# A conv, dynamic-filter and expert block on one core: the matmuls that only keep TensorE busy are taken out

## The reference

```python
x = x + conv_block(layernorm_over_channels(x))
t = tokens(x)
t = t + experts(layernorm(t))
return from_tokens(t)

def conv_block(x):                       # 128 -> 32 -> 128 channels
    xd = relu(group_norm(conv1x1(x, w_scale1)))
    outs = []
    for w, d in zip((w_cata, w_catb, w_catc, w_catd), (1, 4, 8, 12)):
        f = softmax(conv3x3(xd, w, dilation=d), axis=1)       # 9 weights a pixel
        outs.append(sum(shifted(xd, k, d) * f[:, k] for k in range(9)))
    y = relu(group_norm(conv1x1(concat([xd] + outs), w_scale2)))
    return relu(group_norm(conv1x1(y, w_scale3)))

def experts(t):                          # 8 experts, the best 2 for each token
    w, i = top_2(t @ gate_w.T); w = softmax(w)
    return sum over the 2 chosen e of w * (gelu(t @ w1[e].T + b1[e]) @ w2[e].T + b2[e])
```

## Time and profile before

| | |
|---|---|
| median of 3 runs | 345.13 us (343.13 to 347.28) |
| profiled execution | 345.51 us, its span 343.7 us |
| mean granted TensorE clock | 0.903 |
| busy in the span: TensorE, VectorE, ScalarE, GpSimd | 285.0, 182.2, 149.4, 204.6 us |
| matmuls with line L1181 | 66, of 379 to 635 ns each by the trace |

### The profile page before, as it was taken

How to read it: one execution, slowest core, us unless ns; L and a number is a source line. 1 busy time by engine, 2 the same in 40 slices (tenths; PEclk the granted TensorE clock), 3 DMA queues, 4 the chain that set the end, 5 groups by cost and what they waited for, 6 DMA issues and landing times.

```text
span 343.7 us, 4640 instructions
## 1 busy us (share of the span) xinstructions
PE 285.0 (83%) x1446; PEld 200.4 (58%) x1446; DVE 182.2 (53%) x429; ACT 149.4 (43%) x352; POOL 204.6 (60%) x195
## 2 busy tenths in 40 slices
PE   2999979877998664747999999999999999993054
PEld 0245525242343344516898888888888888882032
DVE  3673699999794788989953111121112222312086
ACT  2742321211003578366936655544554454343082
POOL 9300269696870036077576777777777777765271
PEclk9999999996899686668999999999999999998555
DMA  7100000000000003375435556665666556630585
GB/s 298 64 3 0 2 0 0 0 2 0 0 0 2 2 0 154 104 281 168 153 109 167 178 178 173 204 207 178 180 205 200 180 176 210 196 109 31 208 352 188
DMA packets 13768, 41.79 MB, mean 122 GB/s; under 512 B 3121, under 2 KB 3121, under 8 KB 13745
## 3 DMA queue, kind: packets, MB, share of 16 engines
q1 hardware_dynamic: 8640, 29.52, 26.3%
q0 software_dynamic: 4096, 8.40, 7.7%
q10 hardware_dynamic: 1008, 3.59, 2.6%
HBM read 32.05 MB, written 9.44 MB: 121 GB/s over the span
## 4 chain that ended last, share of the span: by engine, by line
PE 63%; DVE 24%; POOL 4%; issue 3%; ACT 3%; DMA 2%; DVEq 0%; POOLq 0%; SPq 0%; ACTq 0%
PE PS L1367 20%; PE PS L1378 20%; PE PS L1242 6%; DVE PRF L846 4%; PE PS L1228 3%; PE PS L1189 3%; POOL RX L451 2%; DVE PRF L1144 2%; DVE st L897 2%; PE PS L1356 2%; PE PS L1389 2%; PE PS L1334 2%; PE PS L1181 1%; DMA SCR<-expert_rows 1%; DVE FE L823 1%
## 5 line engine op out<-in xcount | busy, mean ns | idle before, releaser
L681 ACT ACTIVATE MV<-PS,WE 128x256 f32<-128x256 f32 x156 | 61.1, 474 | 57.5 <-PE PS L1367 57.5
L506 POOL DMA_INDIRECT expert_rows<-RX,dsti x64 | 62.5, 977 | 25.1 <-issue 16.9
L1367 PE MATMUL PS<-SCR,WE 128*128 (+1 forms) x312 | 75.6, 386 | 0.0
L1378 PE MATMUL PS<-MV,WE 128*128 128x256 f32 x312 | 73.7, 379 | 0.0
L458 POOL TENSOR_TENSOR PRF<-PRF 128x1024 f32<-128x1024 f32 x21 | 49.4, 2359 | 40.2 <-DVE PRF L846 38.7
L1378 PEld LDWEIGHTS PS<-MV,WE 128*128 128x128 f32 x312 | 59.0, 190 | 7.8
L1367 PEld LDWEIGHTS PS<-SCR,WE 128*128 128x128 f32 x312 | 57.3, 193 | 6.9 <-issue 0.3
L1104 DVE TENSOR_SCALAR PRF<-PS,WE 128x256 f32 x30 | 14.5, 485 | 80.5 <-PE PS L1378 80.5
L499 POOL DMA_INDIRECT RX<-token_rows,dsti x46 | 44.1, 959 | 14.0 <-issue 13.7
L846 DVE TENSOR_TENSOR PRF<-RX,PS 128x512 f32<-128x512 f32 x66 | 41.7, 677 | 6.0 <-PE PS L1228 5.9
L1228 PE MATMUL PS<-FT,k 72*128 72x512 f16 x72 | 27.4, 403 | 5.2 <-DVE PRF L846 3.6
(11 more groups left out here) (235 smaller groups left out, 376.8 us busy)
## 6 DMA issues: line engine op xcount, KB each, us to landing
WE<-experts SPq DMA_DIRECT2D x39, 514.5 KB
token_rows<-SCR SPq DMA_DIRECT2D x4, 512.0 KB, 3.2
SCR<-expert_rows SPq DMA_DIRECT2D x4, 512.0 KB, 8.1
SCR<-expert_rows ACTq DMA_DIRECT2D x4, 512.0 KB, 8.4
out<-PRF SPq DMA_DIRECT2D x8, 256.0 KB, 2.2
X<-x ACTq DMA_DIRECT2D x2, 512.0 KB, 6.3
X<-x SPq DMA_DIRECT2D x2, 512.0 KB, 8.2
first_token_rows<-SCR SPq DMA_DIRECT2D x2, 512.0 KB, 2.6
```

The lines of the kernel that those rows point to most:

```text
L506: nc.gpsimd.indirect_dma_start(yr, bass.IndirectOffsetOnAxis(ap=dsti[:, 1, q:q + 1].bitcast(U32), axis=0), YS[:, q % NR, :], None).then_in ...
L681: last = nc.scalar.activation(GF[:, j % 2, c * STEP:(c + 1) * STEP], first_layer(j, c), ACT.Gelu, bias=part(j, "b1")[:, c:c + 1])
L1367: last = nc.tensor.matmul(first_layer(j, c), part(j, "w1")[:, c * P:(c + 1) * P], columns, start=True, stop=True)
L1378: last = nc.tensor.matmul(second_layer(j), part(j, "w2")[:, c * C:(c + 1) * C], GF[:, j % 2, c * STEP:(c + 1) * STEP], start=(c == 0), sto ...
```

## The change

All four calls of `keep_busy` and the function itself are taken out; 66 matmuls go. Nothing else changes, and no other instruction changes its order on its engine.

```diff
             per_image(2, WC1[:, :], X, u_done)
 
-            def keep_busy(n, b):
-
-                for _ in range(n):
-                    nc.tensor.matmul(bank(b), k16_("ident"), k16_("sel")[:, 0:HALF], start=True, stop=True)
-
             def logits(d, tap):
...
             pe.wait_ge(c16_in, 16)
-            keep_busy(30, 6)
             pe.wait_ge(wcb_ready, 2 * B)
...
                     if d + 2 < ND and LOGITS_AT[tap] == at:
                         logits(d + 2, tap)
 
-            keep_busy(12, 5)
 
             def third_conv(b, h, first):
...
             nc.tensor.matmul(bank(4, 2 * B), prm_("group"), mv3[:, 0:2, :], start=True, stop=True).then_inc(gm_done, 1)
-            keep_busy(12, 5)
             tokens(0)
             tokens(1)
...
                 one_hot(i + 1, OHQ_A, i, 2 * i, bank(4, 2 * QA), i == 0, i == 1)
-            keep_busy(12, 7)
 
             def ranks():
```

## The result

| | before | after |
|---|---|---|
| median | 345.02 us (4 runs, 343.13 to 347.28) | 348.63 us (4 runs, 346.25 to 349.80) |
| profiled execution, its span | 345.51, 343.7 us | 347.94, 346.1 us |
| mean granted clock | 0.903 | 0.874 |

The ratio is 1.0105 (95% interval 1.0060 to 1.0151, which is 2.1 to 5.2 us): slower by 3.6 us, with 3.0 forecast and 348.1 us against 348.6. The ratios given here leave out executions that lie over 1.5% above the fastest of their kernel (four of the 12 in e1, e5 and e9); their mean granted clock is 0.866 to 0.883, against 0.878 to 0.898 in the others of these three, and that is a part of what is measured, so for the experiments the mean of all executions stands beside the ratio, with twice its standard error.

A forecast was written before the change was run, and what follows sets the result against it. TensorE was taken to bound the experts' stage, so earlier delays add one for one. 1.9 + 0.4 + 0.7 + 0 = +3.0 us on the profiled 345.5 gives 348.5; the median is 0.4 lower, so 348.1 us, range 345.8 to 351.0.

The forecast's parts named there:

- What bounds, and that nothing swallows a delay: Experts, 160 to 310 us: TensorE busy 149.96 of 150 us, so any earlier delay enters the result one for one.
- Place 1: 30 matmuls before the 3x3 convolution: without them the clock falls and the convolution starts at 0.50; +1.9 us (1.3 to 2.7).
- Place 2: 12 matmuls before the third convolution: without them the clock falls before or inside it, even chances; +0.4 us (0 to 0.9).
- Place 3: 12 matmuls before the tokens: without them tokens start sooner, near 118.4 us, but at 0.50; +0.7 us (-0.3 to +2.3).
- Place 4: 12 matmuls before the gather wait and experts: nobody waits for them and the clock falls anyway; 0 us.
- The sum: All four removals together: +3.0 us, giving 348.1 us, 0.9% slower; chance 0.60.
- Time freed at place 3: Rival: place 1's idleness costs no lasting clock, and tokens' statistics start 0.8 us sooner; 344.3 us, chance 0.14.
- The clock low for longer: Rival: late rises, place 2's full 0.9 and place 3 at 0.50 throughout; +5.9 us, 351.0 us, chance 0.14.
- Place 4 holding the clock: Rival: the block before the experts keeps the clock up in most executions; +1.8 us, 349.9 us, chance 0.07.
- The collision of VectorE with GpSimd's addition: Rival: shifted work shrinks or grows a 2.00 us VectorE step; at most 1.7 us either way, 346.4 if gone, chance 0.05.

The follow-up runs named there:

- e1: Kernel before with only the 30 warming matmuls in front of the 3x3 convolution removed; +2.2 +- 1.5 us, ratio 1.0023.
- e5: Kernel before with 10 instead of 30 warming matmuls at the same point ahead of the 3x3 convolution; +2.1 +- 1.5 us, ratio 1.0032.
- e9: Kernel before with the 30 warming matmuls ahead of the 3x3 convolution replaced by 60 of 32 columns; +1.5 +- 1.4 us, ratio 1.0005.
- e12: The changed kernel again, all four warming blocks out, against the kernel before, in 12 executions; +2.7 +- 0.9 us, ratio 1.0084, median 348.12 us.
- e3: Kernel before with only the 12 warming matmuls in front of the tokens removed; +2.3 +- 1.2 us, ratio 1.0075.
- e11: Kernel before with the 12 warming matmuls behind the one-hot products removed and one added behind each of 10 broadcasts; -1.8 +- 0.7 us, ratio 0.9952.

## Why the prediction was right

**What bounds, and that nothing swallows a delay.** Right. The 1.5 us of place 1 was 1.6 at the third convolution and, with place 3's 1.5 added, 3.0 at the experts; Route is 29.3 to 29.7 us in every profile.

**Place 1, +1.9 (1.3 to 2.7).** Right. The three profiles without the block (after, e1, e12) have Conv 1.5, 2.8 and 1.4 us later, mean 1.9; e1's lies 0.1 above the range. That the mean is the forecast's own figure is luck, with three values that far apart. The clock fell as forecast, 3.9 us after the last matmul in the changed kernel.

**Place 2, +0.4 (0 to 0.9).** Right in both ends: 0, 0 and 0.8 us in three profiles. The even chances can't be told better with three.

**Place 3, +0.7 (-0.3 to +2.3).** The mechanism was right (start at 118.4 less shift, at 0.50, the statistics waiting for TensorE), the size too small: 1.5 us between the two profiles, 1.4 between the averages. Two parts of the term were off. The rise in the changed kernel's first profile came 5.9 us behind the tokens' start, later than any of the three rises that I took the 2.6 to 5.4 us from; in e3 and e12 it was 4.6 and 3.6 us, inside them. And the block was judged by one execution, in which it ran at 0.50 to its end; in seven of ten a part of the block ran at 1.00, it was over in 4.2 to 4.4 us instead of 5.3, and Tokens took 14.1 to 14.2 us, 0.9 less than in the profile from which I had made the sum. Against that one profile the three without the block are 1.5, 0.6 and 0.1 us longer, 0.7 on average, just the forecast: what was missed is mostly what the block gives in its better executions.

**Place 4, 0.** Right as far as the times can tell (+0.5 +- 1.3), and the route to the experts is unchanged.

**The sum, +3.0.** Measured 3.6 in the first executions, 2.7 +- 0.9 in e12. The stages give 1.9 + 0.3 + 1.4 = 3.6. That the total came within 0.6 us is partly luck: place 3 was put at half its size, and in the two first profiles Rest gave 0.6 us back, so that their spans differ by 2.4 us only.

**The rivals.** Time freed at place 3: out by e3. The clock low for longer: single parts of it came true (place 1's late end in e1, place 2's in e12), never all three; the highest of the changed kernel's 16 executions is 349.8 us, where this rival had 351.0. Place 4 holding the clock: not seen. The collision of VectorE with GpSimd's addition stayed where it was: the step took 2.01 us after the change too, with tokens and chain shifted together; so what the Trainium skill ("SBUF — State Buffer", SBUF: two separate sides) would make of it in another position wasn't put to the test.

**What the prediction treated too lightly** is the luck of the stages in which nothing changed: one clause for the middle stage, none for the experts' first steps.

## What to carry to other kernels

A warming block is worth what the clock is worth to the work right behind it, if that work is TensorE's and on the chain: look for the last idle time before dense work, and fill it up to the work: here 30 matmuls that did so held the clock, ten early ones, 60 short ones and five late ones did not. A block that ends with its work hidden costs nothing, and one with 4 us of idle time behind it buys nothing. Count a block in time at both levels: its own success halves it, and a split that looks tidy may leave a hole. Where light work lets the clock fall while another engine is the bound, a few full-width matmuls between the light ones may pay as much as a block (1.8 us in e11, with its cause not fully shown); in the stage where TensorE is the bound each costs its full time.

## What the runs showed of the hardware that I had not expected

- The spread of one kernel's executions (342.1 to 349.1 us before, in 105 on three chips) goes with the clock: those under 343 us have a mean granted clock of 0.898 to 0.912, those over 347 us one of 0.879 to 0.889. Without any difference in the program of the stage, Middle took 78.4 to 81.6 us, with dips that began anywhere from 40 to 60 us (none there in before) and from 76 to 81 us, and Rest 188.8 to 192.4 us, by whether the clock rose 2.7 us or 11.7 us behind the experts' first matmul. Both spreads are larger than any of the four prices that were sought, so marks inside the profile told more than the times.
- The time from the start of dense work to the rise was 3.6 us (e12) to 6.2 us (e1) at place 1, where the work had no gaps to speak of. At the experts, with waits of up to 2 us in between, it was 2.7 to 3.8 us in ten profiles and 8.8 to 11.7 in four.
- Sixty matmuls of 32 columns took 1.67 us, 28 ns each: count alone fills little time.
